# Four recurrent layers on one core: layer 3's attention values computed feature-major, with the softmax division on GpSimd

## The reference

```
q, k, v = split(xn @ w_qkv.T)                  # 64 wide each
sim = q @ k.T / 8, causal mask
s = softmax(sim) @ v @ w_out.T + b_out
f = sum over the top 2 of 16 experts of c_e * (silu(xn @ gate_e) * (xn @ up_e)) @ down_e, plus one shared expert
x = x + s * silu(f)
```

## Time and profile before

| | us |
|---|---|
| timed runs, median of 3 (lowest to highest) | 728.08 (726.6 to 734.29) |
| the profiled execution | 722.49 |
| its span, first to last instruction | 720.4 |
| TensorE busy | 634.2 |
| VectorE busy | 409.2 |
| ScalarE busy | 365.3 |
| GpSimd busy | 239.3 |

### The profile page before, as it was taken

The page is one execution under the profiler, slowest core; times in us unless marked ns, Lnnn a source line. Parts: engine busy times, 40 slices in busy tenths (PEclk is TensorE's granted clock), DMA queues, the critical chain, the costliest instruction groups (busy, mean ns, idle before and its releaser), DMA issues.

```text
span 720.4 us, 12207 instructions
## 1 busy us (share of the span) xinstructions
PE 634.2 (88%) x4082; PEld 408.3 (57%) x4082; DVE 409.2 (57%) x892; ACT 365.3 (51%) x845; POOL 239.3 (33%) x226
## 2 busy tenths in 40 slices
PE   6897999985995999988987898899797998899896
PEld 2783535874683766655665644445465665645353
DVE  0847655552431825675486568755676486545643
ACT  4424576422653552457558553355358558644342
POOL 2000172054146000666455522122136324623041
PEclk9997899996998999999999999999999999999999
DMA  8900032443353321100000021030000000021030
GB/s 312 346 1 0 8 106 63 133 139 121 103 156 104 120 70 45 37 20 2 9 19 5 2 81 40 0 119 15 17 1 1 2 1 1 1 76 44 10 124 15
DMA packets 29291, 44.45 MB, mean 62 GB/s; under 512 B 3880, under 2 KB 15888, under 8 KB 28720
## 3 DMA queue, kind: packets, MB, share of 16 engines
q1 hardware_dynamic: 26256, 36.48, 15.3%
q0 software_dynamic: 2976, 7.21, 3.4%
HBM read 34.37 MB, written 9.31 MB: 61 GB/s over the span
## 4 chain that ended last, share of the span: by engine, by line
PE 58%; DVE 17%; issue 8%; ACT 8%; POOL 4%; another core or an unknown queue 4%; DMA 1%; DVEq 0%; ACTq 0%; SPq 0%; POOLq 0%
PE bank L568 54%; ACT arena L1177 6%; POOL arena L2533 2%; DVE arena L2225 2%; POOL arena L2541 2%; DVE arena L2210 2%; PE bank L935 1%; DVE arena L2219 1%; DVE arena L2363 1%; DVE arena L2233 1%; PE bank L1043 1%; DMA x<-in_x 1%; PE bank L749 1%; DVE bank L2261 1%
## 5 line engine op out<-in xcount | busy, mean ns | idle before, releaser
L1177 ACT ACTIVATE arena<-bank 128x512 f32<-128x512 f32 (+8 forms) x224 | 125.7, 565 | 124.4 <-PE bank L568 58.3
L568 PE MATMUL bank<-arena,w 128*64 128x128 f32 (+2 forms) x528 | 146.2, 424 | 9.5 <-ACT arena L1177 6.7
L1177 ACT ACTIVATE arena<-bank,arena 128x128 f32<-128x128 f32 (+1 forms) x244 | 87.8, 386 | 107.4 <-PE bank L568 52.4
L568 PE MATMUL bank<-arena 64*128 64x256 f32 (+8 forms) x832 | 110.7, 331 | 2.4 <-ACT arena L1177 2.2
L568 PE MATMUL bank<-arena,work 128*128 128x128 f32 x624 | 86.1, 285 | 15.6 <-DVE arena L2115 6.0
L568 PE MATMUL bank<-xn_b,w 128*128 128x512 f32 (+1 forms) x192 | 91.9, 602 | 4.0 <-DVE arena L2363 2.5
L568 PEld LDWEIGHTS bank<-arena,work 128*128 128x128 f32 x624 | 78.8, 198 | 27.8 <-issue 25.0
L568 PEld LDWEIGHTS bank<-arena 64*128 64x128 f32 (+4 forms) x832 | 73.9, 170 | 30.5 <-issue 13.4
L568 PEld LDWEIGHTS bank<-arena,w 128*128 128x128 f32 (+1 forms) x528 | 62.2, 164 | 44.3 <-issue 32.3
L2551 POOL TENSOR_TENSOR arena<-arena,w_ew 128x512 f32<-128x512 f32 x32 | 42.3, 1325 | 132.0 <-DVE arena L2374 70.1
L2445 POOL DMA_INDIRECT slots_in<-arena x32 | 33.8, 1056 | 90.5 <-ACT arena L1177 80.9
(11 more groups left out here) (217 smaller groups left out, 882.5 us busy)
## 6 DMA issues: line engine op xcount, KB each, us to landing
work<-in_ew SPq DMA_DIRECT2D x46, 256.0 KB
w_ew<-cw SPq DMA_DIRECT2D x64, 128.0 KB, 2.9
slots_in<-work SPq DMA_DIRECT2D x2, 1472.0 KB, 17.7
arena<-slots_in SPq DMA_DIRECT2D x10, 256.0 KB, 3.7
slots_out<-arena POOLq DMA_DIRECT2D x10, 256.0 KB
w_ew<-in_ew SPq DMA_DIRECT2D x1, 2048.0 KB, 11.8
w<-in_p SPq DMA_DIRECT2D x1, 1840.5 KB, 10.1
w<-in_p SPq DMA_DIRECT2D x1, 1297.0 KB, 10.6
```

Of the source, the lines that this page charges most:

```text
L568: return nc.tensor.matmul(o, lhsT, rhs, start=start, stop=stop, skip_group_check=True)
L1177: return nc.scalar.activation(o, i, f, bias=bias, scale=scale, **kw)
```

## The change

- **Values feature-major.** `values` makes out[64, 128 queries] += v3 block (stationary, 64 columns) times pt3 block (moving, 128 columns). Even key blocks write PSUM partitions 0 to 63, odd ones 64 to 127. The sum of the two halves is left to the projection: `w_out3` has its 64 rows twice, 128 in all, loaded by one more DMA. Chunk 0 of g=0 has an even block only and is projected from 64 rows by a matmul of its own.
- **Division ahead of the transposes.** The batched `scaled()` goes, with the four transposes to feature-major and `ot3`. VectorE's new `sums(c)` makes the reciprocal of each chunk; GpSimd's new `normed(n)` multiplies the exponentials by it in place, a piece of up to 512 keys at a time; `turned` waits for that ("p3s").
- **GpSimd's order.** After `weigh` of units 0, 1, 3 and 5 comes `normed` of chunk 0, 1, 2, 3.
- **The steps.** Scores, maxima and probs at steps 0, 1, 3, 5 (were 0, 2, 4, 6); sums at 1, 2, 4, 6; transposes at 2, 4, 6, 7 (were 1, 3, 5, 7); values at 3, 5, 7, 8 (were 2, 4, 6, 8).
- **The end of a half.** ScalarE copies o3 from its bank and TensorE projects it, at i=9 as before.

```diff
+SCORE3, SUM3 = {0: 0, 1: 1, 3: 2, 5: 3}, {1: 0, 2: 1, 4: 2, 6: 3}
+TURN3, VALUE3 = {2: 0, 4: 1, 6: 2, 7: 3}, {3: 0, 5: 1, 7: 2, 8: 3}
...
-        w_out3 = sb("w_out3", [DK, D])
+        w_out3 = sb("w_out3", [P, D])
...
-                                     ("three", ((w3t[:], p3), (w_out3[:], wout3)))):
+                                     ("three", ((w3t[:], p3), (w_out3[0:DK], wout3), (w_out3[DK:P], wout3)))):
...
-                            pe.wait_ge(*at("e3", n, k))
+                            pe.wait_ge(*at("p3s", n, k))
...
-                                i = mm(ob[:, c * DK:(c + 1) * DK], pt3[:, k, j], v3[:, 4 * k + j],
-                                       start=k == 0 and j == 0, stop=4 * k + j == n)
+                                key = 4 * k + j
+                                i = mm(ob[key % 2 * DK:key % 2 * DK + DK, cs(c)], v3[:, key], pt3[:, k, j],
+                                       start=key < 2, stop=key >= n - 1)
...
-                            o = fresh("quick", "ob3", g)
-                            pe.wait_ge(*at("ot3", g))
-                            for c in range(C):
-                                j = nc.tensor.transpose(o[0:DK, cs(c)], ot3[:, g % 2, c], ident[:])
-                            j.then_inc(*step("ob3", g))
                             o = fresh("slow", "s", 3, g)
                             pe.wait_ge(*at("o3_s", g))
-                            mm(o[:], w_out3[:], o3[:, g]).then_inc(*step("s", 3, g))
+                            if g == 0:
+                                mm(o[:, 0:CT], w_out3[0:DK], o3[0:DK, g, 0:CT])
+                            mm(o[:, (1 - g) * CT:], w_out3[:], o3[:, g, (1 - g) * CT:]).then_inc(*step("s", 3, g))
...
-                            after(("ob3", g))
-                            fn(o3[:, g], psum("ob3", g)[0:DK], ACT.Copy).then_inc(*step("o3_s", g))
+                            after(("o3", g))
+                            if g == 0:
+                                fn(o3[0:DK, g, 0:CT], psum("o3", g)[0:DK, 0:CT], ACT.Copy).then_inc(*step())
+                            fn(o3[:, g, (1 - g) * CT:], psum("o3", g)[:, (1 - g) * CT:], ACT.Copy).then_inc(
+                                *step("o3_s", g))
...
+                    def sums(c):
+                        n = g * C + c
+                        after(("e3", n, (n + 4) // 4 - 1))
                         if g == 1:
+                            v.tensor_tensor(sm3[:, n, 1:2], sm3[:, n, 1:2], sm3[:, n, 2:3], ALU.add).then_inc(*step())
+                            after()
+                        v.reciprocal(sm3[:, n, 5:6], sm3[:, n, 1:2]).then_inc(*step("rc3", n))
...
+                        if i in SUM3:
+                            sums(SUM3[i])
+                        if i in SCORE3:
+                            maxima(SCORE3[i])
...
+                    def normed(n):
+                        for k in range((n + 4) // 4):
+                            keys = slice(k * GT, min(k * GT + GT, (n + 1) * CT))
+                            pool.wait_ge(*at("rc3", n))
+                            nc.gpsimd.tensor_tensor(p3b[:, n % 2, keys], p3b[:, n % 2, keys], sm3[:, n, 5:6].to_broadcast(
+                                [P, keys.stop - keys.start]), ALU.mult).then_inc(*step("p3s", n, k))
...
-                        for k in range(EP3):
-                            weigh(g, k)
+                        for i in range(1, EP3 + 1):
+                            weigh(g, i - 1)
+                            if i in SUM3:
+                                normed(g * C + SUM3[i])
```

More of the change, by code:

```diff
@@ L382, in four_layers @@
         pt3 = take([2, C, P])
-        ot3 = take([2, C, DK])
-        o3 = take([2, GT], DK)
+        o3 = take([2, GT])
         assert used[0] <= spare_b, (used[0], spare_b)
@@ L1004, in entry3 @@
                     if g == 0:
-                        pe.wait_ge(ready["three"], 32)
+                        pe.wait_ge(ready["three"], 48)
                     pe.wait_ge(*at("xn", 3, g))
@@ L1096, in layer3 @@
                             advance(NEXT[i])
-                        if i % 2 == 0 and i // 2 < C:
-                            score(i // 2)
-                        if i % 2 == 1 and i // 2 < C:
-                            turned(i // 2)
-                        if i >= 2 and i % 2 == 0 and i // 2 - 1 < C:
-                            values(i // 2 - 1)
+                        if i in SCORE3:
+                            score(SCORE3[i])
+                        if i in TURN3:
+                            turned(TURN3[i])
+                        if i in VALUE3:
+                            values(VALUE3[i])
                         if i >= 2:
@@ L1657, in layer3 @@
                             advance(NEXT[i])
-                        if i % 2 == 0 and i // 2 < C:
-                            probs(i // 2)
-                        if i % 2 == 1 and i // 2 < C:
-                            turned(i // 2)
+                        if i in SCORE3:
+                            probs(SCORE3[i])
+                        if i in TURN3:
+                            turned(TURN3[i])
                         if i >= 7 and g == 0:
@@ L1664, in layer3 @@
                         if i == len(units):
-                            after(("ob3", g))
-                            fn(o3[:, g], psum("ob3", g)[0:DK], ACT.Copy).then_inc(*step("o3_s", g))
-                            reached[("ob3", g, "read")] = reached[("o3_s", g)]
+                            after(("o3", g))
[3 more added lines that the diff above has]
+                                *step("o3_s", g))
+                            reached[("o3", g, "read")] = reached[("o3_s", g)]
                     gate(3, g, psum("ff", 3, g)[:], 0.0, ("ff", 3, g))
@@ L2277, in layer2_att @@
                     if g:
-                        dve.wait_ge(ready["three"], 32)
+                        dve.wait_ge(ready["three"], 48)
                     for m in range(MB + 2):
@@ L2344, in maxima @@
                                 *step("mx3", n))
-                    def scaled():
-                        cc = slice(g * C, (g + 1) * C)
-                        after(("o3", g))
+                    def sums(c):
+                        n = g * C + c
+                        after(("e3", n, (n + 4) // 4 - 1))
                         if g == 1:
-                            v.tensor_tensor(sm3[:, cc, 1], sm3[:, cc, 1], sm3[:, cc, 2], ALU.add).then_inc(*step())
+                            v.tensor_tensor(sm3[:, n, 1:2], sm3[:, n, 1:2], sm3[:, n, 2:3], ALU.add).then_inc(*step())
                             after()
-                        v.reciprocal(sm3[:, cc, 5], sm3[:, cc, 1]).then_inc(*step())
-                        after()
-                        v.tensor_tensor(ot3[:, g % 2], psum("o3", g)[:, 0:C * DK].rearrange(
-                            "p (c d) -> p c d", d=DK), sm3[:, cc, 5:6].to_broadcast([P, C, DK]),
-                                        ALU.mult).then_inc(*step("ot3", g))
-                        reached[("o3", g, "read")] = reached[("ot3", g)]
+                        v.reciprocal(sm3[:, n, 5:6], sm3[:, n, 1:2]).then_inc(*step("rc3", n))
                     def inner(i, k):
@@ L2390, in layer3 @@
                             advance(NEXT[i])
-                        if i % 2 == 0 and i // 2 < C:
-                            maxima(i // 2)
-                        if i == len(units):
-                            scaled()
+                        if i in SUM3:
+                            sums(SUM3[i])
+                        if i in SCORE3:
+                            maxima(SCORE3[i])
                         for _ in range(ROUTE3_STEPS[g].get(i, 0)):
```

## The result

The changed kernel took 746.13 us (median of 4 runs, 743.78 to 749.11) and the kernel before 731.18 us on the same chip: ratio 1.0205, 95% interval 1.0113 to 1.0296, so 15 us slower (8 to 22). The forecast was 739.5 us, range 729 to 748. In a later call on another chip it was 726.65 against 702.19 us, ratio 1.0401 (1.0316 to 1.0486), which would be 28 us. Some executions of a kernel are slow, over 1.5% above its fastest at a lower clock, among them two of these four (732.9 and 729.0) and the profiled ones of experiments 1, 2, 3, 9 and 11. The other two, 716.47 and 724.3, lie 19.5 us above 700.9, the mean of the five comparable executions of the kernel before, and that is the better figure. The sign is the same on both chips.

The account below looks back on a forecast made before the run. TensorE, busy 88% of the span, was taken as the bound. The terms summed to +11.4 us, taking the profiled 722.49 us to 733.9; with 5.6 us for the timed median the forecast was 739.5 us, range 729 to 748.

Parts of the forecast that it names:

- (c): Chunk 0's transposes wait for GpSimd's division, queued behind the weighing that waits for routed weights, in four halves: +17.2 us.
- (d): Chunk 3's transposes in step 7 wait for GpSimd's division behind weigh(5): +6.3 us over the four halves.
- (e): Other waits in layer 3, some going and some coming, such as for gathered rows: net -0.6 us, bounds -3 and +3.
- (f): TensorE's switches of array shape around sixteen groups of value products: 0 to 1.6 us, +0.8 taken.
- (g): Half-speed TensorE clock stretches behind waits in layer 3: +2.0 us taken, bounds -1.7 and +9.
- (a): Layer 3's value products run as pairs on two column halves, saving 3.5 us a batch: -7.0 us.
- (b): Tail of each half, between the last down matmuls and the output projection, loses scaling and four transposes: net -7.3 us.
- the clock falls at each stall: Rival: six to eight half-speed stretches instead of one, +20 us, 748 us in all; chance 0.17.
- weights arrive in time: Rival: first weighing waits for VectorE, not the DMA, so chunk 0 waits 3 us in all; -6.5, 721.5 us; chance 0.08.
- Batch 0 swallows its stalls: Rival: VectorE partly bounds batch 0, so its TensorE stalls cost half, without clock loss; +3.1, 731 us; chance 0.20.

Follow-up runs that it names:

- experiment 1: The changed kernel with GpSimd's division of each chunk put ahead of the weighing, not behind it; 700.71 us against 705.92 for the kernel before, ratio 0.9976.
- experiment 2: The changed kernel with each half's first weighing using a constant tile, not waiting for routed weights; 706.35 us against 705.92 for the kernel before, ratio 1.0011.
- 3: The changed kernel with the division on VectorE behind the reciprocals, GpSimd only weighing; 711.95 us against 705.92 for the kernel before, ratio 1.0068.
- experiment 9: The kernel before with only the new steps for scores, sums, transposes and values; 734.43 us against 729.41 for the kernel before, ratio 1.009.
- 11: As 10, with the matmul that spreads the factors moved ahead of step 8's value products; 730.39 us against 729.41 for the kernel before, ratio 1.0026.
- experiment 5: The kernel before with feature-major values and split projection, old steps, softmax division left out; 690.9 us against 702.19 for the kernel before, ratio 0.9857.
- experiment 6: As experiment 5, with all key blocks on column half 0 and one 64-row projection; 730.08 us against 729.41 for the kernel before, ratio 0.9999.
- experiment 8: The changed kernel with five dead 128x512 matmuls ahead of the chunk-0 wait in each g=1; 713.7 us against 702.19 for the kernel before, ratio 1.0207.
- 10: The kernel before with feature-major values, old steps, and VectorE multiplying the division factors into the products leaving PSUM; 698.86 us against 705.92, ratio 0.9896.
- 12: The kernel of 10 run a second time, unchanged; 701.9 us against 705.88 for the kernel before, ratio 0.9989.

## Why the prediction was right, and which terms were mis-sized

The sign, the place and the chain were right: the transposes of chunk 0 behind GpSimd behind the DMA, four times, and experiment 1 shows it by undoing just that order. The timed +15 us (8 to 22) holds the forecast +11.4; the stage sums, +20.4 and +19.4, and the second series, +19.5, say that it was low. That the median fell inside the range has luck in it: terms (c) and (d) were 4.8 us too high, (e), (f) and (g) 13.2 too low, and 728.08+20.4 would lie just beyond the upper end, 748. Term by term, in the profiled executions:

| term | forecast | measured | by |
|---|---|---|---|
| (a) products paired | -7.0 | -6.9 | rows of the value groups, experiment 5 against 6 |
| (b) tails | -7.3 | -6.8 | the same rows as in the forecast: 8.6 us before, 1.9 after; projections 0.1 less |
| (f) shape switches | +0.8 | +3.7 | rows of the value groups, experiment 5 against the kernel before, less (a) |
| (c) chunk 0 | +17.2 | +14.9 | four waits above |
| (d) chunk 3 | +6.3 | +3.8 | waits at 461.33, 516.34, 517.34, 681.47, 730.60, 731.60 |
| (g) clock | +2.0 | about +8.5 | 20.3 us busy at half speed against 3.4, halved |
| (e) the rest | -0.6 | about +3.2 | what is left of 20.4 |
| sum | +11.4 | +20.4 | |

(c) came out 2.3 us lower, 1.3 of it because the weights came back sooner, by 0.1 to 0.7 us in each half: in batch 1, g=1 GpSimd started 5.3 us after their write (700.62 to 705.94), where it had been 6.0 (680.10 to 686.12). In (d) batch 1, g=1 came as summed (1.5 forecast), and batch 0, g=0 did not (3.3 forecast, 1.32 at 461.33):

```profile
730.60 0.63 PE L1044 MATMUL bank<-const,arena 128*128 128x128 f32 x4 [1.05 <-POOL arena L2547]
731.60 0.63 PE L1044 MATMUL bank<-const,arena 128*128 128x128 f32 x4 [0.37 <-POOL arena L2547]
```

The term most off is (g). I wrote that the two waits of 5.9 and 6.4 us "should each bring such a stretch (3.4 us)" and took 0.3 for the shorter ones. The two long waits brought stretches of 6.8 us each, and the shorter waits of g=0 did bring stretches: 3.4 us from 660.4 behind a wait of 2.03, and 10.2 us from 445.4 around the waits of 0.95 at 443.35 and 2.58 at 447.06 on VectorE. That is most of the rival "the clock falls at each stall", to which I gave 0.17; its 748 us was nearly the measured time on the first chip. Experiment 8 shows that the clock's part is real: filling the waits with useless matmuls took away the two long stretches, worth 4.4 us. How many short waits bring a stretch is not settled: the one of 2.03 (2.08 in the second trace) did, the one of 1.82 in experiment 8 did not. The upper bound of (g) (+9) held.

In (e) I had seen that waits for the gathered rows would come; experiment 9 shows that the new steps alone cost 7.0 us in the stages, nearly all in batch 0, 4.2 of them clock and 2.8 waits, where I had written -0.6 with +3 as the bound. In the changed kernel the clock's part stands in the row (g).

(a) and (b) held. (f) was too small by 2.9 us: I took 0.05 us a group, the middle between nothing and the 0.10 more that the earlier trace rows shows ahead of one, and counted nothing behind it; a group costs 0.24. (In the earlier trace rows the second row of products starts 0.27 us behind the first, not 0.22; that was a sign of it.)

The rivals: "weights arrive in time" was the state that experiment 2 made by hand, with stage sum +5.8 (+2.4 without the clock) where its sum was -6.5: with the DMA out of the way TensorE still waited 9.7 us in front of transposes (5.5 for ScalarE, 4.2 for GpSimd). Experiment 1, at +0.3, is nearer to it and still not faster. "Batch 0 swallows its stalls" is refuted by the stages: batch 0 grew by 11.1 us and batch 1 by 9.3, and TensorE's waits of (c) and (d) came to 9.3 us in each. The rule of the Trainium skill, "GPSIMD Engine Reference", section Engine selection (VectorE for an elementwise multiply), says which engine and not which place: the division on VectorE has stage sum +7.7, better than on GpSimd behind the weighing (+20.4) and worse than on GpSimd ahead of it (+0.3).

## What to carry to other kernels

When work moves to an idle engine, look at what stands ahead of it in that engine's queue and what that waits for, not only at how fast the engine is or how idle: 13 to 17 us of harmless idling on a DMA became TensorE's own wait, and two swapped lines took it away. Split a change that has two halves before judging it: here the value products won 10 us and the division with its new steps lost 26. And price a wait of TensorE in a dense stretch with the slow clock behind it, which here added about half as much again (8.5 us on 18.7 us of waits).

## What the runs showed of the hardware that was not expected

- A TensorE wait of 2 us in a dense stretch can be followed by matmuls at half clock (660.39: 2.03 us of idling, then PEclk 0.54 for 3.4 us), and filling the two waits of 5.3 and 5.5 us with matmuls whose result is not used made the kernel about 6 us faster (stage sum +19.4 to +13.1). But stretches also come and go without an edit: the kernel of experiments 10 and 12 lost 1.7 us to them in one execution and 5.1 in the other.
- A group of 64-column stationary products between 128-column matmuls costs 0.24 us beyond its products: 0.09 more ahead of the first (0.16 against 0.07) and 0.15 behind the last (experiment 5). Two products on the two column halves in turn took 0.22 us, as one on a single half did (experiment 6).
- A GpSimd multiplication by a broadcast factor, 128x512, took 1.04 us against 0.69 for a like VectorE product: 1.5 times. Back to back, `x2` rows of it are 1.39 (512 and 128 keys) and 1.61 us (512 and 256).
- The same kernel and the same code of the first layers took from 390 to 434 us up to layer 3 on different chips and executions; only stages of the same code on both sides made the experiments comparable to a few us.
